# Four changes of order in the steady loop of a fused attention and FP4 feed-forward kernel

## The reference

```python
xn = _layernorm(x)
q, k, v = heads(xn @ Wq.T), heads(xn @ Wk.T), heads(xn @ Wv.T)   # 16 heads of 16
q, k = q / |q|, k / |k|                                          # L2 norm per head
s = softmax(q @ k.T + alibi + window mask) @ v @ Wo.T            # keys at t .. t+127
gate, up = q4(xn) @ q4(w_gate).T, q4(xn) @ q4(w_up).T            # 704 columns each
g = silu(q4(silu(gate) * up) @ q4(w_down).T)
out = x + s * g
```

## Time and profile before

| | |
|---|---|
| median of 3 runs | 502.65 us |
| profiled execution, its own time | 503.14 us |
| its span, first to last instruction | 501.4 us |
| granted TensorE clock, mean | 0.980 |
| TensorE matmul busy | 451.2 us (90%) |
| VectorE busy | 441.2 us (88%) |
| GpSimd busy | 409.6 us (82%) |
| ScalarE busy | 402.5 us (80%) |
| chain that ended last | PE 53%, ACT 20%, issue 11%, DVE 10% |

### The profile page before, as it was taken

How to read it: one execution, slowest core, us unless ns; L and a number is a source line. 1 busy time by engine, 2 the same in 40 slices (tenths; PEclk the granted TensorE clock), 3 DMA queues, 4 the chain that set the end, 5 groups by cost and what they waited for, 6 DMA issues and landing times.

```text
span 501.4 us, 14045 instructions
## 1 busy us (share of the span) xinstructions
PE 451.2 (90%) x4990; PEld 314.2 (63%) x4990; DVE 441.2 (88%) x897; ACT 402.5 (80%) x584; POOL 409.6 (82%) x897
## 2 busy tenths in 40 slices
PE   0378889999999999999999999999999999999997
PEld 0144556666667666676767676667666766666665
DVE  4989989999989999989989999988998999887686
ACT  1466988988888888888887888888888888888952
POOL 6544678899988888889997898989999888887751
PEclk9857999999999999999999999999999999999999
DMA  8211011224321314223221222222422121222100
GB/s 300 88 43 44 6 37 44 65 75 76 75 63 45 45 41 67 64 64 64 66 65 43 64 34 54 65 54 54 54 54 54 44 24 43 54 54 54 44 22 33
DMA packets 78276, 29.35 MB, mean 59 GB/s; under 512 B 67712, under 2 KB 77696, under 8 KB 78208
## 3 DMA queue, kind: packets, MB, share of 16 engines
q1 hardware_dynamic: 77920, 28.39, 24.7%
q10 hardware_dynamic: 288, 0.08, 0.1%
HBM read 7.49 MB, written 4.19 MB: 23 GB/s over the span
## 4 chain that ended last, share of the span: by engine, by line
PE 53%; ACT 20%; issue 11%; DVE 10%; POOL 3%; DMA 1%; ACTq 0%; DVEq 0%; POOLq 0%
PE gt L351 10%; PE up L351 10%; PE gt L551 9%; ACT probs L1341 8%; PE bank_q L351 8%; PE bank_b L357 5%; ACT L1341 4%; PE gt L573 4%; ACT pv_t L1219 3%; ACT qk_sq L1319 3%; PE bank_b L598 2%; PE scores L505 2%; PE gt L555 1%; DMA qk_slots<-qk_stack 1%; PE gt L357 1%
## 5 line engine op out<-in xcount | busy, mean ns | idle before, releaser
L1341 ACT ACTIVATE probs<-scores 128x1024 f32<-128x1024 f32 (+1 forms) x101 | 102.2, 1012 | 2.3 <-PE scores L505 1.2
L1526 POOL TENSOR_SCALAR_AFFINE_SELECT probs<-probs 128x512 f32<-128x512 f32 x128 | 81.9, 641 | 1.7 <-ACT probs L1341 1.3
L1533 POOL TENSOR_SCALAR_AFFINE_SELECT probs<-probs 128x512 f32<-128x512 f32 x120 | 76.2, 637 | 3.7
L598 PE MATMUL bank_b<-probs,vals 128*32 128x128 f32 x1952 | 59.7, 274 | 0.6 <-DVE vals L944 0.3
L598 PEld LDWEIGHTS bank_b<-probs,vals 128*32 128x32 f32 x1952 | 51.6, 110 | 7.4 <-issue 5.7
L1219 ACT ACTIVATE qk_stack<-bank_q 128x512 f16<-128x512 f32 x64 | 35.1, 595 | 22.3 <-DVE bank_q L923 22.3
L793 DVE SCALAR_TENSOR_TENSOR xT_lo<-gt,xT_hi 128x512 f16<-128x512 f32 (+1 forms) x34 | 22.3, 657 | 26.3 <-ACT xT_hi L1219 26.3
L551 PE MATMUL gt<-wdn_hi,hT_hi 128*128 128x256 f16 x160 | 43.6, 273 | 0.6 <-DVE hT_lo L845 0.6
L551 PE MATMUL gt<-wdn_hi,hT_lo 128*128 128x256 f16 x160 | 43.6, 273 | 0.0
L551 PE MATMUL gt<-wdn_lo,hT_hi 128*128 128x256 f16 x160 | 43.6, 273 | 0.0
L1563 POOL TENSOR_TENSOR h_q<-h_grid,h_scale 128x704 f32<-128x704 bf16 x31 | 43.1, 1391 | 0.0
(11 more groups left out here) (219 smaller groups left out, 1468.5 us busy)
## 6 DMA issues: line engine op xcount, KB each, us to landing
out<-y SPq DMA_DIRECT2D x32, 128.0 KB, 1.9
x_all<-x SPq DMA_DIRECT2D x20, 128.0 KB, 2.0
x_all<-x SPq DMA_DIRECT2D x3, 512.0 KB, 4.1
x_all<-wproj SPq DMA_DIRECT2D x1, 768.0 KB, 6.9
dn_raw<-wd SPq DMA_DIRECT2D x1, 704.0 KB, 8.7
probs<-wg SPq DMA_DIRECT2D x1, 640.0 KB, 5.3
probs<-wu SPq DMA_DIRECT2D x1, 640.0 KB, 7.6
qk_slots<-qk_stack SPq DMA_TRANSPOSE x32, 3.7
```

Of the source, the lines that this page charges most:

```text
L598: done = e.matmul(pv_bank(i)[32 * n:32 * n + 32, grp * P:(grp + 1) * P], va, pr, start=part == 0, stop=part == 1 or final(i))
L1341: e.activation(probs[j % P_BUFS][:, grp, :, side(j), :], score_banks(j, grp)[:, :, :, side(j), :].rearrange("p b e h q -> p (b e) h q"), A ...
L1526: e.affine_select(out=own, in_=own, compare_op=ALU.is_ge, fill=0.0, base=0, pattern=[[0, GRP], [-1, P]], channel_multiplier=1).then_inc(s_ ...
L1533: e.affine_select(out=part, in_=part, compare_op=ALU.is_gt, fill=0.0, base=0, pattern=[[0, GRP], [1, P]], channel_multiplier=-1).then_inc( ...
```

## The change

The instructions stay the same. Their order changes in the loop of 27 turns, on three engines:

```diff
@@ tensor_program, loop for t in range(4, 31)
+                scores(t - 1, 0)
                 tr_x(t + 1)
-                scores(t - 1, 0)
                 scores(t - 1, 1)
@@ vector_program, loop for t in range(4, 31)
                 wide_x(t + 1)
                 rscale_x(t + 1)
+                norm_x(t + 1)
                 lo_x(t + 1)
...
                     ln_moments(t + 3)
+                hidden(t - 2)
                 unit(t)
-                hidden(t - 2)
                 gated(t - 4)
...
                 denom(t - 3)
-                norm_x(t + 1)
                 attend(t - 3)
@@ scalar_program, loop for t in range(4, 31)
                 exp(t, 0)
+                hi_x(t + 2)
                 exp(t, 1)
                 keep_pv(t - 2)
-                hi_x(t + 2)
                 hi_h(t - 2)
```

## The result

The changed kernel takes 535.14 us (median of 6 runs, 532.38 to 538.09) against 502.76 us before: a ratio of 1.0655, 95% interval 1.0634 to 1.0676. The forecast was 527.5 with a range up to 533.0: the right sign, 2.1 us outside the range. The profiled execution took 534.65 us; its span is 532.9.

A forecast was written before the change was run, and what follows sets the result against it. A ring through ScalarE (silu to keep_pv) and TensorE (tr_tail to the next silu) bounds the kernel. 26 turns x (0.45 + 0.47) = 23.9 us, plus 1 for late landings, gave 527.5 us; range 513.5 to 533.

The forecast's parts named there:

- that ring: ScalarE from silu to tr_tail, 5.14 us, then TensorE from tr_tail to the next silu, 8.91 us: said to set the turn.
- the price of `hi_x`: ScalarE: hi_x between the two exponentials makes keep_pv later, adding 0.45 us a turn.
- the price of `hidden` ahead of `unit`: VectorE: unit comes 0.99 us later; less 0.52 us of ScalarE idle time ahead of silu, +0.47 us a turn.
- the sum of both: Over 26 turns, 0.45 us for hi_x plus 0.47 us for hidden ahead of unit: 23.9 us.
- scores* and *norm* at 0 in the regular turn: TensorE's scores ahead of tr_x and VectorE's norm_x ahead of lo_x: each claimed to cost 0 in regular turns.
- The smallest slack that matters is 0.52 us: ScalarE's idle time ahead of silu, claimed as the smallest slack that matters beside the bounding cycle: 0.52 us.
- late DMA transposes: TensorE: scores waiting for late transposes ahead of tr_x delay pv, 0.3 us each; about 1 us, bounds 0 and 8.
- The late chain costs more: Rival, 11%: unit chain held up again, by DMA ahead of tr_x or values before pv; 0.3 us a turn, 535 us.

The follow-up runs named there:

- square: Kernel before with square(t+1) ahead of silu(t-1) on ScalarE: 496.4 us, ratio 0.9877.
- norm: Kernel before with only norm_x(t+1) moved ahead of lo_x(t+1) on VectorE: 502.14 us, ratio 0.9996.
- scores: Kernel before with only scores(t-1,0) moved ahead of tr_x(t+1) on TensorE: 504.07 us, ratio 1.0028.
- scores* undone: Changed kernel with tr_x(t+1) again ahead of scores(t-1,0) on TensorE: 529.37 us, ratio 1.0528.
- hidden: Kernel before with only hidden(t-2) moved ahead of unit(t) on VectorE: 519.26 us, ratio 1.0322.

## Why the prediction was wrong

Right: what bounds the turn (*square* took time out of that ring, *norm* and *scores* alone didn't); the price of `hi_x`, +0.45 forecast, +0.49 measured alone; the price of `hidden` ahead of `unit`, +0.47 forecast, +0.50 alone; the sum of both, 0.92 forecast, 0.93 measured; *scores* and *norm* at 0 in the regular turn. "The smallest slack that matters is 0.52 us" missed the second ring, 0.25 us under the first. The sum did not suffer, since both edits with a price lengthen the turn. Off by a little: the turn at the change of batch lost 1.16 and not 0.9, 0.2 us in all.

The step that failed is a term of the sum: late DMA transposes, "A few such landings make about 1 us in all". It measured 5.8 us against the kernel with *scores* undone, and 6.6 us in the profiled execution. Four things were wrong in it, and a fifth in the range. First and largest, `pv` was put at 1.9 us behind the wait, at TensorE's full clock; in two of the seven late turns the clock fell and it took 3.3. That the clock could fall in the loop was not in the working at all. It makes about 3.2 of the 6.6 us. The kernel before gave no sign of it, as its stretch of the 26 turns shows (columns as above, the clock is the 1.00):

```profile
92.66:457.23 364.57, 350.08 (x4000) 248.05 (x3999) 331.75 (x673) 312.39 (x442) 327.48 (x724) 1.00 0.27 56
```

Second, seven turns in 26 were late, not a few. The row gave only minimum, median and maximum, and I didn't list the 32: before, too, seven of the loop's transposes took 4.7 to 5.6 us. Third, one landing lies above the 5.6 us of that row: 6.29 in this execution. Fourth, a landing of 5.6 us at full clock cost 0.58 (the turn of 15.56) and not 0.3: from the start of the scores to `pv` it was 1.23 (444.85 to 446.08) where 1.10 had been put for the way from the landing on. And fifth, the range was drawn too tightly: the term's own upper bound was 8 us, which puts the forecast at 534.5, and the range stopped at 533.

The Trainium skill ("TensorE: Matmul & The Clock Gate", section "HAM oscillation — how this bites in real kernels") describes a kernel in which each wait for a DMA, of some 3 to 5 us, throttles TensorE again, and the next matmuls run at half the clock. The trace agrees in kind: 0.90 mean granted clock over the turn of 17.92 us, 1.00 over the regular ones. It differs in size: the waits here are 1.21 to 2.42 us, and two of the seven cost the clock. So the page names what the working left out, but wouldn't have said which turns pay.

The rival "The late chain costs more" named the place, the DMA ahead of `tr_x`. That its 535 us are the measured time is chance: it priced 0.3 us in every turn, where the loss is in seven of 26, half of it by the clock.

## What to carry to other kernels

Find the ring, price each edit by what it adds to the ring, and count what sticks out over the next ring: that gave 0.92 us a turn for 0.93. Then look at every wait on a DMA that an edit puts ahead of other work, take the whole list of its landings rather than the median, and ask what TensorE does during the late ones, since an idle time can cost again in clock. An edit that costs 1.2 us alone can cost 5.8 when another has made its data later: *scores* puts the wait for q and k in front, and *hidden* makes them late.

## What the runs showed of the hardware

The late transposes go together with a packet on the queue that the profile calls "instruction". Over the 54 transposes of the loop in the profiles of before and after, 18 had such a packet in their first 3.6 us: 17 of them landed after 3.9 to 6.3 us. Of the 36 without one, none took over 3.75. Over all seventeen profiles it is 139 of 153 with a packet that took 3.9 us or more, and none of the 306 others that took over 3.8. The DMA view of the changed kernel, 116.7 to 122.5 us (GB/s in 40 slices, then the queues and the issue):

```profile
GB/s 0 0 0 0 0 0 0 0 0 0 0 0 0 0 0 0 0 0 0 0 0 0 210 260 267 240 26 0 0 0 0 0 0 0 4 7 11 9 9 11
...
q8 instruction: 1, 0.02, 1.9%
...
qk_slots<-qk_stack SPq DMA_TRANSPOSE x1, 6.3
```

A quarter of the transpose moves, then next to nothing moves for about a microsecond, and the rest follows after the stretch shown. That the packet causes the pause was not tested; the runs show only that they come together.
